# A hybrid block on one core: attention's k, v and q projections as seven products of 384 columns, their operands prepared in the first feed-forward

## The reference, cut to what matters

```
x: (8, 256, 512), added to in place by four stages
  attn_a   : a stack of 4 small layers of width 64 (norms, a long convolution, a small MLP)
  ffn      : layernorm, then gate/up (512 -> 1792), silu(gate)*up, down (1792 -> 512);
             each weight is w * (su @ sv) with rank 4
  attn_b   : on layernorm(x): 32 query heads and 8 key/value heads of 128
             q = x @ Wq.T   k = x @ Wk.T   v = x @ Wv.T
             q, k = rmsnorm over the 128 of a head (times q_norm_w, k_norm_w)
             softmax(q k^T / sqrt(128) + alibi, causal) v, then @ Wo.T
  ffn      : the same weights once more
```

## Time and profile before

| | us |
|---|---|
| median of 3 runs (lowest, highest) | 2506.8 (2497.2, 2507.6) |
| the profiled execution | 2500.7 |
| its span (first to last instruction) | 2499.4 |
| TensorE busy (matmuls) | 2413.7 |
| VectorE, ScalarE, GpSimd busy | 1501.7, 994.7, 721.0 |

### The profile page before, as it was taken

One profiled execution on the slowest core, in us unless ns is written; L12 is line 12 of the kernel. 1 busy time (PEld: TensorE's weight loads), 2 busy tenths in 40 slices (PEclk: granted clock), 3 DMA queues, 4 the chain that ended last, 5 costly groups with the idle time before them and its releaser, 6 DMA issues. The chain is left out here.

```text
span 2499.4 us, 39181 instructions
## 1 busy us (share of the span) xinstructions
PE 2413.7 (97%) x13194; PEld 2040.9 (82%) x13194; DVE 1501.7 (60%) x3769; ACT 994.7 (40%) x2642; POOL 721.0 (29%) x1226
## 2 busy tenths in 40 slices
PE   6799999999899999999999999999999979999999
PEld 4577778888778888888888888888888868887887
DVE  7766665221377666666666666666666656565554
ACT  6433322111154554545545545455455442122112
POOL 4530342000033433434434334344343330011000
PEclk9899999999999999999999999999999979999999
DMA  4235469555200000100000001000000005555554
GB/s 141 95 142 194 183 218 313 202 201 193 87 26 1 18 27 1 43 1 18 26 1 18 26 1 43 1 18 27 1 18 22 1 33 199 197 200 183 191 190 152
DMA packets 60357, 228.33 MB, mean 91 GB/s; under 512 B 6456, under 2 KB 13752, under 8 KB 49408
## 3 DMA queue, kind: packets, MB, share of 16 engines
q1 hardware_dynamic: 58800, 224.37, 25.1%
q10 hardware_dynamic: 1360, 1.46, 0.2%
HBM read 184.91 MB, written 40.89 MB: 90 GB/s over the span
## 5 line engine op out<-in xcount | busy, mean ns | idle before, releaser
L714 PE MATMUL psum<-wkvq_h,axT_h 128*128 128x256 f32 (+1 forms) x1024 | 360.9, 352 | 1.5 <-DVE axT_l L2028 1.5
L2003 POOL TENSOR_SCALAR prob<-prob,rsum 128x128 f32<-128x128 f32 (+1 forms) x512 | 213.7, 430 | 465.0 <-DVE rsum L2101 450.9
L714 PE MATMUL psum<-wkvq_h,axT_l 128*128 128x256 f32 (+1 forms) x1024 | 346.0, 338 | 0.0
L714 PE MATMUL psum<-wkvq_l,axT_h 128*128 128x256 f32 (+1 forms) x1024 | 345.8, 338 | 0.0
L1946 ACT ACTIVATE prob<-biased,nmax 128x256 f32<-128x256 f32 (+1 forms) x512 | 227.6, 446 | 240.8 <-DVE nmax L2091 240.6
L714 PE MATMUL psum<-wo_h,oT_h 128*128 128x512 f32 x512 | 212.6, 415 | 0.0
L714 PEld LDWEIGHTS psum<-wkvq_h,axT_l 128*128 128x128 f32 x1024 | 194.7, 190 | 21.6
L714 PEld LDWEIGHTS psum<-wkvq_h,axT_h 128*128 128x128 f32 x1024 | 195.0, 190 | 17.7 <-issue 1.9
L714 PEld LDWEIGHTS psum<-wkvq_l,axT_h 128*128 128x128 f32 x1024 | 195.5, 191 | 15.9
L714 PE MATMUL psum<-wo_h,oT_l 128*128 128x512 f32 x512 | 201.4, 393 | 0.0
L714 PE MATMUL psum<-wo_l,oT_h 128*128 128x512 f32 x512 | 200.4, 391 | 0.0
(11 more groups left out here) (297 smaller groups left out, 5978.5 us busy)
## 6 DMA issues: line engine op xcount, KB each, us to landing
wgu<-weff_gu SPq DMA_DIRECT2D x42, 1024.0 KB, 5.7
wD<-weff_dn SPq DMA_DIRECT2D x56, 512.0 KB, 4.6
wS<-weff_s SPq DMA_DIRECT2D x28, 1024.0 KB, 6.9
wdn<-weff_dn SPq DMA_DIRECT2D x42, 512.0 KB, 3.3
weff_gu<-wgu SPq DMA_DIRECT2D x14, 1024.0 KB, 4.2
wA<-weff_gu SPq DMA_DIRECT2D x28, 512.0 KB, 4.2
stage<-in_wqkv SPq DMA_DIRECT2D x16, 768.0 KB, 4.3
stage<-in_ffn_w SPq DMA_DIRECT2D x14, 768.0 KB, 5.5
```

Of the source, the lines that this page charges most:

```text
L714: ins = pe.matmul(out_ap, stat[a], mov[b], start=start and n == 0, stop=stop and n == last)
L2003: pool.tensor_scalar(prob[:, b, lo:hi], prob[:, b, lo:hi], rsum[:, b, t:t + 1], 1.0, ALU.mult, ALU.mult).then_inc(prob_done, 1)
```

## The change

The projections of a unit are a product of 256 x 512 rows with 512 x 768 weights (k, v and four q heads). Rows are cut into two tiles (128) by two halves of the inner dimension, weights into two inner halves by two column halves: the weights' columns are ordered k, q 0, q 1 | v, q 2, q 3. Seven products (1, 6, 7, 5, 2, 4, 3), each 6 matmuls of 384 columns, are added up by Winograd's scheme: p1 copied by ScalarE, then u2, u3, c22, u4, c11, c21, c12 on VectorE, the four results in SBUF (`cc`).

The operands are the blocks and sums of blocks: 7 row parts per sequence and 7 weight sets per group, each split in high and low. Weight sets of all 8 groups and row parts of sequences 0 to 5 are made in phase 1 (`projection_steps`) and stored to DRAM (`weff_q`, `weff_x`); sequences 6 and 7 are made in units 4 and 5. Phase 2 loads row parts for every unit (two slots) and the weight sets per group (eight slots). Squares are made head by head from `cc` with running sums; the reductions on VectorE are gone; GpSimd also scales the q of tile 1. `out` 0 is cut in two: `outa` (heads 0, 1) stands ahead of `at` 1.

```diff
+        def projection_steps(o):
+            left = [("xadd", s, SJ - 1) for s in range(NS)]
+            for g in range(KVH):
+                o.add(("qf", g, 0), "sp", 0.7, [("qlo", g - 1, 0), ("qcomb", g - 1, 0)] if g else left + [("slo", 2 * IC - 1, 0)], 7)
+                o.add(("qcomb", g, 0), "pool", 8.2, [(("qf", g, 0), 7.0)] + ([("qlo", g - 1, 1)] if g else []), 7)
+                for part in range(2):
+                    before = [(("qsv", g, 0), 6.0)] if part else [(("qsv", g - 1, 1), 6.0)] if g else []
+                    o.add(("qhi", g, part), "act", 3.2 if part else 2.5, before + [("qcomb", g, 0) if part else (("qf", g, 0), 7.0)], 7)
+                    o.add(("qlo", g, part), "dve", 3.3 if part else 2.6, [("qhi", g, part)], 7)
+                    o.add(("qsv", g, part), "sp", 1.4, [("qlo", g, part)], 7)
+            for q in range(SEQS1):
...
+                o.add(("acomb", q, 0), "pool", 3.2, [("aev", q, j) for j in range(STILES)], 6)
+                o.add(("ahi", q, 0), "act", 2.1, [("acomb", q, 0)] + ([(("asv", q - 1, 0), 6.0)] if q else []), 6)
+                o.add(("alo", q, 0), "dve", 2.1, [("ahi", q, 0)], 6)
+                o.add(("asv", q, 0), "sp", 1.4, [("alo", q, 0)], 6)
...
-        first.add(("kvq", 0, 0), "sp", 1.4, [("slo", 2 * IC - 1, 0)], 9)
+        projection_steps(first)
...
+        SET = KC // 2 * KVQ // 2
+        PRODUCTS2 = (1, 6, 7, 5, 2, 4, 3)
+        def act_group(g, part):
...
+            if g == 0 and part == 0:
+                stack_left(act)
+            else:
+                act.wait_ge(s_out, 32 * (IC + 2 * g + part))
+            for dst, src in group_parts(part, q_hl[0]):
+                ins = act.activation(dst, src, ACT.Copy)
+            ins.then_inc(gu_hi, 1)
...
+                elif what == "qsv":
+                    sp.wait_ge(gu_lo, 2 * IC + 2 * a + b + 1)
+                    cols_ = slice(3 * SET, 7 * SET) if b else slice(0, 3 * SET)
+                    for part in range(2):
+                        sp.dma_start(weff_q[a][:, part, cols_],
+                                     q_hl[part][:, 0:(3 + b) * SET].bitcast(F32)).then_inc(s_out, 16)
...
@@ phase1_over
-            engine.wait_ge(gu_lo, 2 * IC)
+            engine.wait_ge(s_out, 32 * (IC + 2 * KVH))
+            engine.wait_ge(xs_out, 32 * SEQS1)
...
@@ order2
+        def products(n, *ms):
+            steps = []
+            for m in ms:
+                j = PRODUCTS2.index(m)
+                steps += [("pr", n, m)] + loads_after(n, j)
+                if m == 4:
+                    steps += [("nrm", n, 1), ("ksc", n, 0), ("qsc", n, 1)]
+                elif m == 3:
+                    steps += [("nrm", n, 0), ("vlo", n, 0), ("qsc", n, 0)]
+            return steps
...
             order2.append(("norm", u, GRP - 1))
...
+            if nxt:
+                order2 += products(u + 1, 1, 6, 7)
...
             order2 += [("pT", u, 0), ("pT", u, 1)]
...
-                order2.append(("q", u + 1, 0))
+                order2 += products(u + 1, 5, 2, 4)
...
             order2 += [("at", u, 0), ("pT", u, 2), ("pT", u, 3)]
...
+            if nxt:
+                order2 += products(u + 1, 3)
...
-            order2.append(("at", u, 1))
+            order2 += [("outa", u, 0), ("at", u, 1), ("out", u, 0)]
             if nxt:
-                order2 += [("qsc", u + 1, 1), ("kT", u + 1, 0), ("qT", u + 1, 0)]
+                order2 += [("kT", u + 1, 0), ("qT", u + 1, 1), ("qT", u + 1, 0)]
             order2.append(("out", u, 1))
...
@@ ScalarE
+                elif what == "pr" and b == 1:
+                    act.activation(pr1[:], region2(1), ACT.Copy).then_inc(p1_done, 1)
+                elif what == "pr" and b in SQUARES2:
+                    name, tile, half = {5: ("c22", 1, 1), 2: ("c11", 0, 0), 4: ("c21", 1, 0), 3: ("c12", 0, 1)}[b]
...
+                    for hd in range(GRP // 2):
+                        n = SSQ[tile] + half * GRP // 2 + hd
+                        ins = act.activation(squares[:, n, :], cc[:, tile, half, (hd + 1) * HD:(hd + 2) * HD], ACT.Square,
+                                             accum_out=ss[:, n:n + 1])
+                    if half == 0:
+                        ins = act.activation(squares[:, tile, :], cc[:, tile, 0, 0:HD], ACT.Square, accum_out=ss[:, tile:tile + 1])
@@ VectorE
+                elif what == "pr" and b == 6:
+                    dve.tensor_tensor(su2[:], pr1[:], region2(6), ALU.add).then_inc(c_done, 1)
+                elif what == "pr" and b == 7:
+                    dve.tensor_tensor(su3[:], su2[:], region2(7), ALU.add).then_inc(c_done, 1)
+                elif what == "pr" and b == 5:
...
+                    dve.tensor_tensor(cc[:, 1, 1, :], su3[:], region2(5), ALU.add).then_inc(c_done, 1)
+                    dve.tensor_tensor(su4[:], su2[:], region2(5), ALU.add).then_inc(c_done, 1)
...
                 elif what == "ksc":
-                    dve.wait_ge(k_rs, a + 1)
+                    dve.wait_ge(r_done, 2 * a + 1)
@@ GpSimd
+                elif what == "nrm":
+                    part = slice(0, SSQ[0]) if b else slice(SSQ[0], SSQ[0] + GRP)
+                    pool.wait_ge(sq_done, squared(a, 4 if b else 3))
...
+                    pool.tensor_tensor(rr[:, part], ss[:, part], mneg_half[:, 0:part.stop - part.start],
+                                       ALU.pow).then_inc(r_done, 1)
+                elif what == "qsc" and b == 1:
+                    pool.tensor_tensor(q_heads(1), *q_scaled(1), ALU.mult).then_inc(q_sc1, 1)
@@ TensorE
-                    for hd in range(GRP):
+                    for hd in range(0, 2) if what == "outa" else range(0 if b else 2, GRP):
                         pe.wait_ge(oT_lo, 2 * a + hd // 2 + 1)
```

More of the change, by code:

```diff
@@ L166, in ordered, with hybrid_block @@
         return order
-def hybrid_block(nc, x_in, win, vecs, b1, w1, w2, wout, bout, ffn_w, lr_long, lr_short, wqkv, wo, qk_w, out, weff_gu, weff_dn, weff_s):
+def hybrid_block(nc, x_in, win, vecs, b1, w1, w2, wout, bout, ffn_w, lr_long, lr_short, wqkv, wo, qk_w, out, weff_gu, weff_dn, weff_s, weff_q, weff_x):
     with ExitStack() as ctx:
@@ new lines, in dve_sequence @@
+        def dve_sequence(what, q, j):
+            if what == "arow":
+                t = q * STILES + j
+                if q < SEQS1:
+                    wait_row(dve, (what, q, j))
+                else:
+                    dve.wait_ge(wo_lo, 2)
+                    if j or q > SEQS1:
+                        dve.wait_ge(a_tile, A_TILE["axT", q, j] - 1)
+                dve_rows(sequence_row(q, j), 2, t).then_inc(a_dve, 1)
+            else:
+                dve.wait_ge(a_act, A_ACT["ahi", q, 0])
+                _, _, hi, lo = sequence_memory(q)
+                for (h, src), (l, _) in zip(sequence_parts(q, hi), sequence_parts(q, lo)):
+                    ins = dve.tensor_tensor(l, src, h.bitcast(F32), ALU.subtract)
+                ins.then_inc(a_dve, 1)
@@ new lines, in pe_sequence, with act_sequence @@
+        def pe_sequence(q, j):
+            if q < SEQS1:
+                wait_bank(("axT", q, j))
+            else:
+                wait_spare(("axT", q, j))
+            bank, row = sequence_bank(q, j), sequence_row(q, j)
+            pe.wait_ge(a_dve, A_DVE["arow", q, j])
+            for k in range(KC):
+                ins = pe.transpose(psum[:, bank, k * P:(k + 1) * P], row[:, k * P:(k + 1) * P], ident[:])
+            ins.then_inc(a_tile, 1)
+        def act_sequence(what, q, j):
+            f, t, hi, _ = sequence_memory(q)
+            if what == "aev":
+                act.wait_ge(a_tile, A_TILE["axT", q, j])
+                if q in (0, SEQS1):
+                    stack_left(act)
+                else:
+                    act.wait_ge(a_dve, A_DVE["alo", q - 1, 0])
+                act.activation(f[:, j, :, :], psum[:, sequence_bank(q, j), :].rearrange("p (k c) -> p k c", k=KC),
+                               ACT.Copy).then_inc(a_act, 1)
+            else:
+                act.wait_ge(a_comb, 4 * (q + 1))
+                if q < SEQS1:
+                    act.wait_ge(xs_out, 32 * q)
+                else:
+                    act.wait_ge(qkv_mm, len(PRODUCTS2) * (q - 1))
+                for dst, src in sequence_parts(q, hi):
+                    ins = act.activation(dst, src, ACT.Copy)
+                ins.then_inc(a_act, 1)
@@ new lines, in hybrid_block, with multiplied @@
+        A_ACT = counts(k for k in order1["act"] + order2 if k[0] in ("aev", "ahi"))
+        A_TILE = counts(k for k in order1["pe"] + order2 if k[0] == "axT")
+        SUMS2 = ("u2", "u3", "c22", "u4", "c11", "c21", "c12")
+        SQUARES2 = (5, 2, 4, 3)
+        REGION2 = {1: KV, 2: KV, 6: WO, 7: QB[0], 4: QB[0], 5: QB[1], 3: QB[1]}
+        OPERANDS2 = {1: (0, 0), 2: (1, 1), 3: (6, 2), 4: (2, 6), 5: (3, 3), 6: (4, 4), 7: (5, 5)}
+        def multiplied(n, m):
+            return len(PRODUCTS2) * n + PRODUCTS2.index(m) + 1
@@ L1688, in wait_spare, with summed, squared, region2 @@
```

(19 more changed lines are left out.)

510 lines of the change are left out of this document (287 added, 223 removed).

## The result

The changed kernel takes 2989.3 us (median of 4, 2983.3 to 2990.1); the kernel before, on the same chip, 2503.9. Ratio 1.194, 95% interval 1.190 to 1.197: 19% slower. The direction was predicted, the size was not: 2806 (2600 to 2900) was forecast.

The account below looks back on a forecast made before the run. The prediction took TensorE, busy 97% of the span, to bound the kernel. 2500.7 + 205 (attention units, product savings included) + 105 (first feed-forward) - 5 (the rest) = 2806 us, range 2600 to 2900.

Parts of the forecast that it names:

- The clock: Attention stage: with two stalls of 2 us TensorE stays 82% busy, so full clock was expected and no time added.
- The stalls: Attention stage: TensorE waits twice a unit for VectorE's oT_l ahead of `wo` matmuls, 2.0 and 2.3 us.
- Part 1: TensorE's products in attention: 42 matmuls of 384 columns at 0.179 us save 1.05 us a unit, 66 us over 63 units.
- Part 2: Attention stage: VectorE's queue order and the norms' chain stall TensorE; 23.95 us a unit, +205 us over 63 units.
- The chain up to the power of six: Norms in a unit: c21 made from 9.5 us, ScalarE's squares to 11.1, GpSimd's power of six to 12.7.
- the first stall: Attention unit: `outa` on TensorE waits for head pair 0's oT_l from 12.0 to 14.0 us, 2.0 us.
- The second stall: Attention unit: after `at` 1, `out` 0 waits for head pair 1's oT_l from 16.45 to 18.75 us, 2.3 us.
- The rival: Attention stage: 1.5 us of columns per unit at half clock, 95 us more; total 2900 to 2960, chance 0.08.
- Part 3: First feed-forward: 67.6 MB more DMA traffic, 113.2 in all, lengthens it by 105 us, at the least 66, at most 150.
- its own sign of error: The prediction called itself wrong if phase 1 ended before 725 us or a unit took under 21 us.
- stores are dearer: First feed-forward's DMA: a stored MB costs 3.4 us, a loaded one 2.7, making 345 us, +109.
- Part 4: Intro before unit 0's scores a few us longer, row transposes leaving attention a few less: together -5 us (-15 to +10).

Follow-up runs that it names:

- experiment 3: Changed kernel with k's scaling behind product 3, q tile 0's scaling behind `at` 1, both tiles' `wo` products cut in two and reordered: 2572.8 us, ratio 1.027.
- experiment 1: Changed kernel with GpSimd's scaling of tile 1's q moved behind the second norm, no longer beside VectorE's ksc: 2965.7 us.
- experiment 2: Changed kernel with 11 and 9 unused matmuls of 512 columns ahead of the two waits for oT_l in each unit: 2902.3 us.
- Experiment 4: Changed kernel storing 192 elements a partition of each weight part: 2940.3 us; with reordered scalings and `wo` products too, 2532.1; with GpSimd's weight sums also cut, 2525.1.

## Why the prediction was wrong, point by point

Two terms failed, both in the attention stage, which was put 210 us too low (+205 for +414.5). The clock was put at nothing and costs 1.6 us a unit. And the step `ksc`, taken at 0.6 us from a row of the kernel before, took 1.49, since GpSimd's scaling beside it was counted as free. The stalls themselves were where they were put. The terms one by one:

**Part 1, right.** 0.179 us was taken for a matmul of 384 columns; 0.178 is measured, the 42 of a unit take 7.6 us for 7.5. TensorE's own work is 19.84 us a unit against 19.65. In experiment 3, with the stalls gone, the unit is 20.3 for 20.7: the gain is real, and the 66 us of 63 units shrink to some 25, then to nothing by longer units where a group begins (1330.3 for 1328.5).

**Part 2, the mechanism of the stalls right, one link mis-sized.** Both stalls are where they were put, with the releasers named. The chain up to the power of six came out within a tenth: c21 made from t = 9.5 (9.5 was written), the power done at 12.8 (12.7). Then `ksc` was taken at 0.6 us, from k_tok's row: it measured 1.49, because in the kernel before that operation read k from PSUM, and here it reads `cc` in SBUF while GpSimd scales tile 1. That the part counted GpSimd's scaling as free, since it "lies in its idle time", was the fault: GpSimd was idle then, but VectorE had both of its tensors to read from SBUF. This is the 1.0 us of the first stall (3.0 for 2.0; experiment 1). The second stall measured 2.56 for 2.3; the power of four took 1.26 us where r_q's row gave 1.01.

**The clock, the term that was left at nothing.** "Two stalls of 2 us leave TensorE busy 82%, so I expect full clock." TensorE is busy 81% of 900 to 2000 us, and the clock is 0.91. The rival had the price almost right, 95 us; experiment 2 measures 87 by the total, 90 in the attention stage, 1.6 us in a typical unit. It belonged in the forecast beside the stalls, not in place of them. The earlier trace rows held the hint on which it should have weighed more: half rate once, after the engine had been idle for part of 5 us. In sum a unit was 19.65 + 4.3 + 0 = 23.95; it is 19.84 + 5.56 + 1.6 = 27.0. That is 193 us over 63 units (about 80 from the stalls, 100 from the clock, 12 from TensorE's own work), and the units at the groups' ends add 16.

**Part 3, the mechanism right, too dear.** ScalarE's waits for the stores, the DMA share (0.93 to 665 us) and the extension were there, but 61.5 us, below the 66 called the least; its own sign of error, an end of phase 1 before 725, stayed away by less than a microsecond. What failed is "stores are dearer", 3.4 us a MB from the earlier trace rows: the stretch 429 to 665 moved 374 GB/s at 0.93 busy, 402 when full, with loads and stores mixed, and 428 in 660 to 680 (busy share 1.02). At 402 the 113 MB take 282 us, 46 more than 236 and not 66. Why the stretch 360 to 420 of before came to only 335 when full, no run shows. The prediction said that the trace agrees with 358 rather than with the 425 GB/s that the Trainium skill ("DMA: Bandwidth & Descriptors", "Bandwidth") gives for one core; the kernel after shows 428 over 20 us, which agrees with the higher figure, and the row at 368 in the earlier trace rows was no ceiling. Experiment 4 splits the 61.5: 39 are the weight parts' stores, 8 go with GpSimd's sums, 15 are open.

**Part 4, wrong in sign.** -5 was written for intro and row transposes; +12 came: TensorE waits 11.9 us for 2.6 MB and 3.9 us for a set queued behind another 1.8 MB.

Together: 193 + 16 - 43.5 + 17 = 182.5 us, and 2987.4 is 183 above the forecast's 2499.4 + 305. That it is not 226 is luck: part 3, too dear by 43.5, hid as much of what the attention stage was too cheap by.
